# New hand-out orders for five engines in a two-layer attention and expert kernel

## The reference

```python
x = L0_attn_x
xn = _layernorm(x, axis=-1)
s = _L0_attn_ref(xn, ...)     # four sublayers: LN, q/k/v, Hamilton products of quaternions
                              # (x, difference, roll, cos x), spectral filter, projection, MLP with Gelu
g = _silu(_L0_ffn_ref(xn, ...))       # 8 experts of 256, top 2, sigmoid gates
x = x + s * g
xn = _layernorm(x, axis=-1)
s = _L1_attn_ref(xn, ...)     # 16 heads of 64, windows of 128 tokens with one window back, rotary, softmax
g = _silu(_L1_ffn_ref(xn, ...))       # 32 experts of 64, top 4 in 2 of 4 groups, and a shared expert
x = x + s * g
```

## Time and profile before

| What | Value |
| --- | --- |
| Median of 3 runs | 4817.23 us (4806.15 to 4819.19) |
| Profiled execution | 4814.87 us, span 4813.1 us |
| Mean granted TensorE clock | 0.949 of full speed |
| PE / PEld busy | 4264.2 us (89%) / 2603.9 us (54%) |
| DVE / ACT / POOL busy | 3833.5 (80%) / 3274.9 (68%) / 1996.1 us (41%) |
| ACT_TABLE_LOAD in front of line 776 | 265, 1283 ns each |

### The profile page before, as it was taken

How to read it: one execution, slowest core, us unless ns; L and a number is a source line. 1 busy time by engine, 2 the same in 40 slices (tenths; PEclk the granted TensorE clock), 3 DMA queues, 4 the chain that set the end, 5 groups by cost and what they waited for, 6 DMA issues and landing times. The chain is left out here.

```text
span 4813.1 us, 75678 instructions
## 1 busy us (share of the span) xinstructions
PE 4264.2 (89%) x20208; PEld 2603.9 (54%) x20208; DVE 3833.5 (80%) x8946; ACT 3274.9 (68%) x6140; POOL 1996.1 (41%) x2033
## 2 busy tenths in 40 slices
PE   5669899898998989899898998989889898998979
PEld 3435555565554555555564554555555564555555
DVE  4779798887978879798887978889798887979853
ACT  2447677676776767677676776767777676777745
POOL 1234344344444444444443434444344443434423
PEclk8779999999999999999999999999999999999989
DMA  4001111111101101111111101101111111111100
GB/s 126 16 25 30 27 30 33 26 32 27 30 25 31 39 21 31 28 29 31 29 31 31 28 23 33 36 21 31 30 28 31 30 31 31 27 27 32 34 20 21
DMA packets 144530, 149.37 MB, mean 31 GB/s; under 512 B 27748, under 2 KB 107932, under 8 KB 143960
## 3 DMA queue, kind: packets, MB, share of 16 engines
q1 hardware_dynamic: 144088, 144.19, 11.5%
HBM read 22.45 MB, written 4.19 MB: 6 GB/s over the span
## 5 line engine op out<-in xcount | busy, mean ns | idle before, releaser
L644 POOL TENSOR_TENSOR s_h<-s_h,ge 128x512 f32<-128x512 f32 x512 | 696.9, 1361 | 1319.2 <-ACT ge L654 1076.0
L952 DVE TENSOR_TENSOR acc<-acc,tmp 128x512 f32<-128x512 f32 x768 | 610.6, 800 | 10.1
L952 DVE TENSOR_TENSOR tmp<-comps 128x512 f32<-128x512 f32 x768 | 605.4, 790 | 8.4
L776 ACT ACTIVATE s_h<-bG 128x512 f32<-128x512 f32 x528 | 314.8, 596 | 434.9 <-DVE hu L1139 226.5
L1371 PE MATMUL bC<-hu,w_d 128*128 128x512 f32 x1056 | 565.3, 617 | 15.7 <-DVE hu L1139 15.7
L753 ACT ACTIVATE probs<-bT,nmax 128x256 f32<-128x256 f32 x1024 | 410.8, 476 | 201.7 <-DVE nmax L1100 199.8
L631 POOL TENSOR_TENSOR rot<-rot,sinT 128x512 f32<-128x512 f32 x256 | 338.1, 1321 | 427.6 <-DMA rot<-raw 426.2
L1100 DVE TENSOR_REDUCE nmax<-bT 128x2 f32<-128x512 f32 x512 | 335.5, 685 | 225.8 <-PE bT L1284 225.2
L1326 PEld LDWEIGHTS bT<-V,probsT 128*128 128x128 f32 x3584 | 430.6, 192 | 101.4 <-issue 56.6
L1139 DVE TENSOR_TENSOR hu<-bU,s_h 128x512 f32<-128x512 f32 x528 | 361.4, 684 | 153.8 <-PE bU L1364 79.5
L1326 PE MATMUL bT<-V,probsT 128*128 128x65 f32 x3584 | 438.7, 274 | 26.7 <-ACT probsT L654 25.6
(11 more groups left out here) (201 smaller groups left out, 9482.7 us busy)
## 6 DMA issues: line engine op xcount, KB each, us to landing
rot<-raw SPq DMA_DIRECT2D x1024, 64.0 KB, 2.0
comps<-comps SPq DMA_DIRECT2D x384, 120.0 KB
x_ld<-in_L_attn_x SPq DMA_DIRECT2D x66, 128.0 KB, 2.2
comps<-comps SPq DMA_DIRECT2D x384, 8.0 KB
out<-O SPq DMA_DIRECT2D x16, 256.0 KB, 2.7
w_a<-in_L_attn_W_qkv SPq DMA_DIRECT2D x1, 1536.0 KB, 14.6
w_fc<-in_L_attn_fc_w SPq DMA_DIRECT2D x1, 1024.0 KB, 9.9
w_g<-in_L_ffn_w_gate SPq DMA_DIRECT2D x1, 1024.0 KB, 5.7
```

The costliest lines, as they stand in the source:

```text
L644: nc.gpsimd.tensor_tensor(s_h[:, :], s_h[:, :], ge[:, :], ALU.mult).then_inc(weighed, 1)
L776: nc.scalar.activation(s_h[:, :], bG[:, :], ACT.Silu).then_inc(silu, 1)
L952: V_.tensor_tensor(dst, i0, i1, op).then_inc(ham[h], 1)
```

## The change

The five words of `ORDER` are replaced. Nothing else is changed: the streams, the steps, what a step does on each engine, its waits and its buffers stay. The words have the same length and the same number of each letter. Of PE's 347 places in the word 191 hold another step than before, of ACT's 309 places 160, of DVE's 315 places 170, of POOL's 99 places 32, and of SP's 43 places 19; no step moves by more than 11 places. The new words are said to come from a new search over several sets of durations with random lateness.

```diff
 ORDER = {
-    "pe": "uuauababatuuububutuututuutuuuuuuuuttutuuttauauututtttuauuauatauauatbuuabauatauutubububbtubtbtuuu"
+    "pe": "uuauabaubauutbtuubuuutttuuutuutuuuuuuttuutuuttuaatutuatuauuatauauatbuuauabauatutbutbubtbubtbtuuu"
...
-    "sp": "aabbattttbaatatbbttbaattabbbttattabbaattbbt",
+    "sp": "aabbbttattaattabbtbtaatatbbtbtatatbbttababt",
```

More of the change, by code:

```diff
@@ L126 @@
 ORDER = {
-    "pe": "uuauababatuuububutuututuutuuuuuuuuttutuuttauauututtttuauuauatauauatbuuabauatauutubububbtubtbtuuu"
[L128 to L139, removed]
+    "pe": "uuauabaubauutbtuubuuutttuuutuutuuuuuuttuutuuttuaatutuatuauuatauauatbuuauabauatutbutbubtbubtbtuuu"
+          "utuutbttbubtutuabtuatuttutatatatauattatutttuutttuauatbuabaututututbububububtbtuutututubtbttbtabu"
+          "atuautttuuauattuatauatuatttbutbuuttbtuatautbtbtabtbtbuatbtutttutbttbubuubtauutttttatubutttutbtuu"
+          "utuutuuutuutuututututuauutatuttbuubtttaubauabtbabuabtabtbta",
@@ new lines @@
+    "act": "uuaabaaabuabaaataabbububbbbbttutuuutauttutbatuttttubatuaaaatuuauaaaaaaaatuabbatbtbabutauttuttbtb"
+           "tbubbubbttbbtbbuttaataabtattttttuubtatuuaauaaaaaataauttubbabtbbuuattttbttbubbubbttbbbbabtubbutau"
+           "attaauattttttuutbtaaubbttbtaabatbtuaatattttaaabtbtbbabuubbbbabtutbtbatbttubttttuuuutturutututtut"
+           "utttuttabaabbababtabu",
+    "dve": "abatbutaabauababuababaubauaatuaabattababuababattaabubabtbbburtbaaubartbbaaubrraaaauaaatabatbaaub"
+           "attaraauatbatbaaturabbbbbbbtbbbtbtbattuabtbatbubtbabbaubaaaaauaaaaaattbbaauttbataabatbauatbbbbat"
+           "ubbbbbbbbbttbbbttbuatabbtautbatatbbtttubtaaaabbaaatubtbbbaababttabattbubabataturbaurabtuababttbu"
+           "babbtbataburbrbatbutttbtbaa",
@@ L140 @@
+    "pool": "abutabuabuautututuutbauttuauabauubtaubbtutatbutauauabtuutbatbubtaubuabutattatutabbbautbbtuututuu"
             "uab",
-    "sp": "aabbattttbaatatbbttbaattabbbttattabbaattbbt",
+    "sp": "aabbbttattaattabbtbtaatatbbtbtatatbbttababt",
 }
```

## The result

The changed kernel took 4675.62 us (median of 4 runs, 4671.39 to 4679.13), the kernel before 4815.24 in the runs beside it. The ratio is 0.9712, 95% interval 0.9695 to 0.9729: 140 us faster.

The account below looks back on a forecast made before the run. The prediction took a round as a chain passing between engines, with no single engine the bound throughout. Its terms summed to −1.60 us per round, × 15 = −24.0 us, giving 4793 us, range 4748 to 4848.

Parts of the forecast that it names:

- A: Start of the round: xn1_T and a cosine come later, delaying VectorE's first quaternion product; cost 0.80 us per round.
- B: Attention scores of pair 0: TensorE's 1.67 us wait for hidden.5 before weight.6 goes; −0.23 us per round.
- C1: Gelu of layer 0: half b's cosine behind gate.8 needs no table load, hidden.8 wait shrinks; −0.73 us per round.
- E: Half a's q cosine between pair 0's scores brings two table loads, mostly hidden; cost 0.50 us per round.
- C2: Scores of pair 1: cosine behind gate.12 without a load, VectorE's 1.12 us wait shrinks; −0.73 us per round.
- C3: Layer 2: cosine behind gate.19, one table load fewer, shorter TensorE and VectorE waits; −0.81 us per round.
- D: Next batch's input: both score maxima directly behind the normalisation, whose own wait stays; −0.40 us per round.
- First and last round: Outer rounds, where only some streams run and load counts stay at 16 and 15; set to nothing.
- The collision rival: VectorE operations held by GpSimd ones: a third more gives 4848 us (chance 0.09), a third less 4738.
- Nothing measurable: Rival for the whole round: stalls removed come back before the next full engine; 4817 us, chance 0.22.

Follow-up runs that it names:

- spin_after: Changed kernel plus dummy matmuls in TensorE's three longest waits (ahead of a:ln1_T.0, weight.6 and S.0.0): 4656.81 us, ratio 0.9683 to the kernel before.
- c2_only: Kernel before, with the new orders on all engines only from 70 to 125 us of a round: 4796.39 us, ratio 0.9967.
- s2_only: Kernel before, with the new orders on all engines only between 125 and 210 us of a round: 4787.84 us, ratio 0.9944.
- no_collision: Kernel before, with one added wait holding GpSimd's rope 7 product until the second half's normalised rows are written: 4800.93 us, ratio 0.9974.
- stop_after: Changed kernel with one added wait: TensorE begins b:prep_T only after ScalarE has read the scores of S.6.0: 4714.47 us, ratio 0.9802 to the kernel before.
- spin_before: Kernel before, with five dummy matmuls while TensorE waits for the normalised rows ahead of b:prep_T, orders unchanged: 4779.33 us, ratio 0.9924.
- three_fixes: Kernel before, with two VectorE maxima directly behind the normalisation, GpSimd's product kept off it, and three dummy matmuls in TensorE's wait: 4748.84 us, ratio 0.9870.
- s3_only: Kernel before, with the new orders on all engines only from 210 us of a round: 4744.06 us, ratio 0.9851.
- s1_only: Kernel before, with the new orders on all engines only for the first 125 us of a round: 4809.28 us, ratio 0.9991.

## Why the prediction was wrong, step by step

- **A, B, C1, E**: +0.34 forecast. In the mean of eleven rounds the stretch is 0.3 us longer, in the round shown 1.03. That the mean meets the sum is luck in part: the stretch also has 3.1 us more half clock than before, which no term holds, and with nearly all half clock gone there (spin_after) it is 2.9 us shorter. The single tells were less good than the sum. A: the first quaternion product was to wait some 2 us and waits 0.40; but the two angle steps ahead of it wait 0.84 and 1.62 us, before 0.32 and 0.31, so the three together wait 1.00 us more, which is A's upper bound. B: TensorE's wait before weight.6 was to go, and is 1.55 (1.67 before), with 2.03 us behind it for GpSimd's Kk. C1: VectorE's wait of 1.16 us is gone, as told. E: hart.0 starts 51.4 us behind the seam and not before 47.6, so by its own tell E was to be wrong; yet the transposes PT.0.0 don't wait and TensorE no longer idles 2.23 us there. The tell was bad, since the step was placed later.
- **C2**: priced at VectorE's waiting for TensorE, because the load is hidden otherwise. The stretch gave 2.88. TensorE had five stops of 0.56 to 1.30 us there, of which I counted two, and its idle time shrinks from 4.04 to 2.23 us. c2_only shows that the size belongs to the new orders from 70 to 125 us and needs nothing ahead of them; that most of it is lost again unless the orders behind it fit, I had not thought of.
- **C3**: −0.81 forecast, −1.45 measured, and its sign and place were right (s2_only). All of VectorE's 0.87 went and TensorE idles 1.4 us less.
- **D**: the failed step. "The longer wait before that, for the normalisation, stays as it is: the steps in front of it come to the same on VectorE." I compared the steps of one engine. The wait is the difference between TensorE's coming and VectorE's coming, and both moved: TensorE has a:prep_T and with it q.7 and down.25 in other places, so q.7 begins 4.85 us ahead of the normalisation and not 5.69, its DMA lands later against it, and GpSimd's product no longer begins with the normalisation. In the changed kernel TensorE's wait is 0.95 us and not 2.49; 1.0 us of this is the collision (no_collision has 1.45). And I priced a stop at its length alone, with the granted clock of 0.74 standing in the earlier trace rows in a window that holds other stops of TensorE; in stop_after a stop 1.43 us longer cost 3.0 us. The runs give three terms: keeping TensorE busy in the stop (22 us beyond the collision, spin_before against no_collision), the collision (12) and the second stop (12). In one run, three_fixes, they are worth 64 us, more than their sum and near s3_only's 70, but behind V.5 they give 3.9 us a round of its 5.0. What makes the other 1.1, of which 0.67 lie behind V.7, is open. One thing that differs there and was not tried alone: the normalisation of the first half also meets a GpSimd product in the kernel before and takes 1.5 us in the mean, in the changed kernel 0.6.
- **First and last round** were set to nothing. The first gave some 6 us (15 ahead of the first output sum, of which one loop round is 9) and the last took 3.
- **The collision rival** held by its own tell, in its better direction: the means left 780 to 810 ns downwards, and (22 + 60) × 768 = 63 us of its 177 went, a third. Its 4738 for that case was right in sign, but it was weighed by the sum of held time: s1_only has 44 us of the 63 and is 5 us faster, and no_collision has one place that is worth 12 us. That one wait took this collision away also shows that not every one is bound to the layout of the work.
- **Nothing measurable**, "stalls that go inside a stretch come back before the next engine that is full", is what s1_only did (V.2 to V.3 gave 2.5 us back). Here it held for a new order that ends in an old one.

The Trainium skill (TensorE: Matmul & The Clock Gate, HAM oscillation — how this bites in real kernels) counts a stretch at half clock as half its length lost. No pair of runs here has that price by itself. For each us of half clock spin_after gives 0.17 us and the step from no_collision to spin_before 0.2 to 0.3, both less than the page's half; stop_after gives 0.4 when its longer stop counts in full, and more when it doesn't. Had I used the page's half at D, the 10 us behind the stop would have read, as an estimate, as at most 5 us a round, 75 us, and one of the cases would have stood near 4720.

## What to carry to other kernels

Look for a low granted clock in the windows behind each stop of TensorE before pricing a stop: here a 1.4 us longer stop cost 3.0 us, and filling the wait with dummy matmuls went with 34 us without a change of order. Before such a gain is put down to the clock, look at what else moved: there a collision of VectorE and GpSimd had gone too, and 22 us are left beyond what its removal gives. In a kernel whose engines run fixed lists, a wait moves when either side moves, so compare when both arrive, with the transfers that hang on them. And a list is good only with its partners: one engine's new order alone cost 2.5 to 2.9%, where all five gained 1.5%.

## What the runs showed that was not expected

- The half clock can move instead of going: spin_before has some 9 us less at 235 us of a round, 3 us more at 210 and 2 us more at 41.
- Held VectorE time tells little of run time: 44 us less of it for 5 us (s1_only), 15 us less at one place for 12 us (no_collision: the mean of that normalisation over 68 is 546 and not 765 ns). Dummy matmuls on TensorE alone took away the same 15 us (spin_before, 546 ns too).
- Parts don't add up: 5 + 26 + 70 us against 140; and behind 210 us of a round TensorE's new order alone loses 142 us, VectorE's alone 121, the two 18, and with ScalarE's they gain 73.
